# Second attention of a graph network: the edge weight's share of the value as a VectorE term instead of a one-row product

## The chip, the cores and the metric

The kernel runs on one core of a Trainium2 chip. The metric is the device time of one launch in microseconds (us). The program is hand-ordered: each engine (PE = TensorE, PEld = its weight loads, DVE = VectorE, ACT = ScalarE, POOL = GpSimd, SP = SyncE, which issues most DMAs) runs its own list of instructions, and semaphores tie the lists together.

## What is computed

The reference runs two graph layers over 50,000 nodes with 128 features and 12,500 edges. The change lies in the second of two transformer convolutions of the first network. Cut to what matters:

```python
q = (h @ Wq + bq).reshape(n, HEADS, C)
k = (h @ Wk + bk).reshape(n, HEADS, C)
v = (h @ Wv + bv).reshape(n, HEADS, C)
e = (edge_attr @ We).reshape(-1, HEADS, C)      # edge_attr: (12500, 1), We: (1, 128)
k_j = k[src] + e
alpha = einsum('ehc,ehc->eh', q[tgt], k_j) / sqrt(C)
a = softmax of alpha over the edges that share a target
msg = (v[src] + e) * a[..., None]
out = segment_sum(msg, tgt)
```

The edge attribute is one number per edge, so `e` is an outer product: the edge's weight times the 128 numbers of We. It enters twice, in the key and in the value.

## The kernel before

The program is a chain of phases with a barrier between them: first dense layer, first attention (from 487 us of the span), second dense layer, second attention (from 1076 to 1400 us), last dense layer, last edge stage. The change touches the second attention alone, `attention(..., l=1)`.

An attention works on the 12,500 edges in 25 chunks (C) of 500 (CH), with features on the 128 partitions and edges along the free axis. Edges are sorted by target. `edge.hd` and `edge.hs` hold, for all 25 chunks, the features at the target and the source of each edge. The second attention has three parts:

1. **The gather pass** (1082.8 to about 1256 us). For chunk k POOL issues four indirect DMAs (`gather`, L1134) that fetch the source rows into `rows` (a ring of U = 4 buffers). PE turns them (`turn`, L210), ACT copies them into `hs[:, k]` (L1364), PE multiplies by Wq and Wk (`query_key`, L1291 and L1292), ACT evicts the query (L1369), and DVE makes the key with its edge share and the product of query and key (`product`, L1416 and L1421). PE sums the products per head into one accumulating bank (`score`, L1297). PE also makes the value (`value`): the product with Wv (L1305) and, onto it, the product of We with the chunk's weights (L1306), which has one contracted row, `ew`, a [1, 500] row loaded by SP. ACT evicts the value with its bias over `hs[:, k]` (L1373).
2. **The softmax** across all edges (about 1256 to 1275 us), a serial chain of DVE instructions that begins with the scan at L1493 and needs the last score.
3. **The output pass** (1275 to 1400 us): weights spread to 128 partitions, times the value, running sums, gate, skip and the store. The value is read from `hs[:, k]`, since EARLY = 25 for l = 1.

The order in each engine's list comes from `steps(n, stages)`: at step t it runs every stage with its lag, so a stage with lag 1 handles chunk t - 1. In the gather pass PE's list is

```python
steps(C, [(0, turn), (1, query_key), (2, score), (1, value)])
```

so step t turns chunk t, but makes key, query and value of chunk t - 1. DVE's list has `product(t)`, then a piece of set-up work for the softmax (`prepare`, for t = 1 to 14; `count`, for t = 15 to 17). SP's list for chunk k is: `load_index` (L1228, the 2 KB of node numbers that POOL's gather k needs), `load_weights_wide` (L1236, the chunk's weights broadcast to 128 partitions, 250 KB, into the ring `ewb` of 4 slots), `store_hd` (L1231, 250 KB), `load_weight` (L1241, the [1, 500] row). `load_weights_wide(k)` first waits until slot k - 4 has been read. SP works through its list in order, so whatever stands behind a waiting entry waits too; `hold` is the wait:

```python
def load_weights_wide(k):
    q = k % U
    hold(sp, ph.seen, m.kj, made(k - U))
    sp.dma_start(ewb[:, q], weight_row(a, k).to_broadcast([128, CH])).then_inc(ewb_loaded[q], 16)
```

In the traces `att_run_cont<-in_edge_weight` is the wide load (ewb is a view of run_cont), `att_dx` is the key kj, `att_prod` its product with the query, and `att_bank` any of the eight PSUM banks. Both attentions have the same names and lines; the stretch tells them apart.

Of the kernel before, what the change touches and what calls it, by code (L numbers as in the profile page):

```python
# [19 lines left out]
ALU = mybir.AluOpType  # L20
# [7 lines left out]
CH = TILE * TILES  # L28
# [16 lines left out]
def made(k):  # L45


    return k + AHEAD + 1
# [67 lines left out]
def hold(sp, seen, sem, value):  # L116

    sp.wait_ge(sem, value)
    sp.sem_inc(seen, 1)
# [1026 lines left out]
def steps(n, stages):  # L1146

    for t in range(min(0, min(lag for lag, _ in stages)), n + max(lag for lag, _ in stages)):
        for lag, stage in stages:
            if 0 <= t - lag < n:  # L1150
                stage(t - lag)
# [20 lines left out]
def attention(nc, a, w, scratch, l, edge):  # L1172
# [4 lines left out]
    U, C = 4, ECHUNK  # L1177
    EARLY = C if l else 10
    with phase(nc, f"att{l}") as ph:
        hd, hs = edge.hd, edge.hs  # L1180
        ew = ph.sb("ew", [1, U, CH])
        qs, prod = ph.sb("qs", [128, 2, CH]), ph.sb("prod", [128, 2, CH])
# [9 lines left out]
        vs, pv = qs, prod  # L1192
        ewb = run_cont[:, :, 0:CH]
        o, sig, dx = (ph.sb(n, [128, 2, CH]) for n in ("o", "sig", "dx"))
        yd = edge.hs
        kj = dx
# [10 lines left out]
        else:  # L1207
            rows = ph.sb("rows", [TILE, U, TILES, D])
        hd_stored, yd_stored = ph.count("hd_stored"), ph.count("yd_stored")
        names = "xT hs qk qs kj prod score weight spread v vs pv o xz gated xo sig dx gx y yn ystats"  # L1210
        m = Group(**{n: ph.stage(n + "_made") for n in names.split()})
        compact, shifted, exps_made = (ph.count(n) for n in ("compact_step", "shifted", "exps_made"))
        counted, rcnt_stored = ph.count("counted"), ph.count("rcnt_stored")
        LAST = C - 1
        with nc.Block() as block:
            @block.sync
            def _(sp):
                ph.start(sp)
                sp.wait_ge(made_first, 1)
                for h in range(HEADS):  # L1220
                    sp.dma_start(cont[32 * h:32 * h + C], compact_flags(scratch)).then_inc(win_loaded, 16)

                def load_index(k):

                    q = k % U
                    if k >= U:
                        hold(sp, ph.seen, idx_loaded[q], 16 * (k // U))
                    sp.dma_start(idx[:, k], index_slot(scratch.src_row if l else scratch.end_index, k * CH)).then_inc(idx_loaded[q], 16)  # L1228

                def store_hd(k):  # L1230
                    sp.dma_start(cols_of(scratch.hdT, k * CH), hd[:, k]).then_inc(hd_stored, 16)  # L1231

                def load_weights_wide(k):
                    q = k % U
                    hold(sp, ph.seen, m.kj, made(k - U))
                    sp.dma_start(ewb[:, q], weight_row(a, k).to_broadcast([128, CH])).then_inc(ewb_loaded[q], 16)  # L1236

                def load_weight(k):
                    q = k % U
                    hold(sp, ph.seen, m.v, made(k - U))  # L1240
                    sp.dma_start(ew[:, q], weight_row(a, k)).then_inc(ew_loaded[q], 16)  # L1241

                def load_cont(k):
                    q = k % U
                    hold(sp, ph.seen, m.yn, made(k - U))
                    if k < U:
                        hold(sp, ph.seen, m.kj, made(LAST))
                    sp.dma_start(run_cont[:, q], cont_window(scratch, k * CH)).then_inc(cont_loaded[q], 16)

                def late_weight(k):  # L1250
                    if k >= EARLY:
                        load_weight(k)

                def late_cont(k):
                    if k >= U:
                        load_cont(k)

                def store_yd(k):
                    hold(sp, ph.seen, m.yn, made(k))
                    sp.dma_start(cols_of(scratch.ydT, k * CH), yd[:, k]).then_inc(yd_stored, 16)  # L1260

                steps(C, [(0, load_index), (0, load_weights_wide)] + [(0, store_hd), (0, load_weight)] * l)
                if l == 0:
                    steps(U, [(0, load_weight)])
                    steps(U, [(0, load_cont)])
                    for k in range(U, EARLY):
                        load_weight(k)
                if l == 1:
                    sp.wait_ge(counted, 1)
                    sp.dma_start(scratch.rcnt.rearrange("o (c e) -> (o c) e", e=CH), bwd[0:C]).then_inc(rcnt_stored, 16)  # L1270
                steps(C, [(0, load_cont), (4, store_yd)] if l else [(0, late_weight), (0, late_cont)])
                for q in range(U):
                    sp.wait_ge(moved[q], 16 * TILES * len(range(q, C, U)))
                if l == 1:
                    sp.wait_ge(hd_stored, 16 * C)
                    sp.wait_ge(yd_stored, 16 * C)

            @block.tensor
            def _(pe):
# [19 lines left out]
                def value(k):  # L1299
                    if EARLY <= k < EARLY + 2:  # L1300
                        pe.wait_ge(m.qs, made(LAST))
                    ps = (psE if k < EARLY else psV)[k % 2]
                    pe.wait_ge(ew_loaded[k % U], 16 * (k // U + 1))
                    pe.wait_ge(m.vs, made(k - 2))
                    pe.matmul(ps[:, 0:CH], w.Wv[:, l], hs[:, k], start=True, stop=False)  # L1305
                    pe.matmul(ps[:, 0:CH], w.We[:, l], ew[:, k % U], start=False, stop=True).then_inc(m.v, 1)  # L1306

# [94 lines left out]
            def _(dve):  # L1402
# [9 lines left out]
                def product(k):  # L1412
# [8 lines left out]
                    dve.scalar_tensor_tensor(out=prod[:, s], in0=kj[:, s], scalar=w.bk[:, l:l + 1], in1=qs[:, s],  # L1421
                                             op0=ALU.add, op1=ALU.mult).then_inc(m.prod, 1)

                def across(values, z, keep, op):

                    after(dve.transpose(tr[:, 0], values[:, 0:32]))
                    after(dve.transpose(tr[:, 1], values[:, CH - 32:CH]))
                    after(dve.tensor_tensor(tr[:], tr[:], near_mask[:] if op == ALU.max else near[:], ALU.add if op == ALU.max else ALU.mult))
                    first, none = (ALU.add, -BIG) if op == ALU.max else (ALU.mult, 0.0)
                    after(dve.tensor_tensor_scan(z[:, 0, 30::-1], keep[:, 0, 31:0:-1], tr[:, 0, 31:0:-1], none, first, op))  # L1430
                    after(dve.tensor_tensor_scan(z[:, 1, 1:32], keep[:, 1, 0:31], tr[:, 1, 0:31], none, first, op))
                    after(dve.transpose(tr[:, 0], z[:, 0]))
                    after(dve.transpose(tr[:, 1], z[:, 1]))
                    return tr[:, 1, 31:32], tr[:, 0, 0:1]
# [49 lines left out]
                        dve.reciprocal(bwd[:], run[:]).then_inc(counted, 1)  # L1484

                before = None
                steps(C, [(0, product), (0, prepare)] + [(0, count)] * l)

                score = psS[:, 0:CH]
                dve.wait_ge(m.score, made(LAST))  # L1490
# [21 lines left out]
                def weigh(k):  # L1512
                    s = k % 2
                    dve.wait_ge(m.spread, made(k))
                    dve.wait_ge(m.vs, made(k))
                    dve.tensor_tensor(pv[:, s], psB[s][:, 0:CH], hs[:, k] if k < EARLY else vs[:, s], ALU.mult).then_inc(m.pv, 1)

                def total(k):
# [336 lines left out]
```

## Time and profile before

| | |
|---|---|
| median of 3 runs | 2256.45 us (2256.12 to 2262.39) |
| the profiled execution | 2257.61 us, its span 2255.8 us, granted TensorE clock 0.951 |
| busy share of the span | PE 87%, DVE 73%, ACT 58%, POOL 52% |
| gather pass of the second attention | 1082.8 to 1256 us |
| POOL's gathers there (L1134) | x100, 1286 ns each, 1.58 us from one to the next |
| products with one contracted row there (L1306) | x50, 630 ns each |

A matmul of f32 data appears as two instructions, so x50 is 25 products. A duration is one instruction's; the time beside an arrow (<-) is the idle time that ended with that release. Idle time of an engine costs only where nothing else is as late.

### The profile page before, as it was taken

How to read it: one execution, taken by the hardware profiler on the slowest of the kernel's cores; microseconds unless marked ns; L12 is line 12 of the kernel's file. 1: busy time of each engine (PE TensorE's matmuls, PEld its weight loads, DVE VectorE, ACT ScalarE, POOL GpSimd, SP SyncE). 2: the span in 40 equal slices, each digit the busy share in tenths (PEclk: the TensorE clock that was granted, in tenths of full speed). 3: DMA queues.
4: the chain of work that ended last, by engine and by line, in shares of the span. 5: the costliest groups of instructions: out<-in, count | busy, mean ns of one | idle time of the engine just before them, and what ended most of it. 6: DMA issues, size and time to landing. Idle time of an engine off the chain costs nothing. (4 is left out here: it accounts for less than half of the span.)

```text
span 2255.8 us, 32073 instructions
## 1 busy us (share of the span) xinstructions
PE 1955.5 (87%) x7584; PEld 1106.6 (49%) x7584; DVE 1643.9 (73%) x3493; ACT 1311.6 (58%) x2509; POOL 1181.4 (52%) x919
## 2 busy tenths in 40 slices
PE   3899999989996888888588696699999999699997
PEld 2444444444332444444233232477777777355554
DVE  6799999967798899999223698577777775355553
ACT  3688888852222677777233111677777775466562
POOL 7466566428840433333688000555555556578885
PEclk9899999999898999999789799799999999799999
DMA  7888888744122999999444133999999995744441
GB/s 173 249 260 254 257 254 254 235 142 96 33 50 79 321 363 356 374 368 327 125 122 115 47 101 103 287 317 331 310 324 323 317 326 188 176 119 117 115 107 30
DMA packets 289533, 476.30 MB, mean 211 GB/s; under 512 B 85811, under 2 KB 162496, under 8 KB 289223
## 3 DMA queue, kind: packets, MB, share of 16 engines
q1 hardware_dynamic: 239124, 441.09, 61.9%
q0 software_dynamic: 46400, 33.03, 7.2%
q8 instruction: 64, 1.05, 0.2%
q14 instruction: 121, 0.99, 0.1%
q10 hardware_dynamic: 3824, 0.13, 0.1%
HBM read 272.11 MB, written 202.60 MB: 210 GB/s over the span
## 5 line engine op out<-in xcount | busy, mean ns | idle before, releaser
L389 POOL DMA_INDIRECT first_x<-in_x,first_index x200 | 261.2, 1306 | 160.8 <-ACT first_xn L583 83.6
L1007 POOL TENSOR_TENSOR last_xh<-last_xin,last_hin 125x512 f32<-125x512 f32 x100 | 127.1, 1272 | 213.4 <-DMA last_xin<-in_x 197.1
L785 POOL DMA_INDIRECT second_entry<-node_map,second_si x100 | 130.8, 1308 | 198.4 <-DVE second_src_row L800 171.7
L1091 PE MATMUL last_psH<-last_g,W2a 128*128 128x500 f32 x400 | 187.8, 592 | 21.1 <-DVE last_hid L1053 20.9
L1100 PE MATMUL last_psO<-W2b,last_hid 128*125 128x128 f32 x1600 | 190.9, 273 | 0.0
L1100 PEld LDWEIGHTS last_psO<-W2b,last_hid 128*125 128x125 f32 x1600 | 182.5, 188 | 0.9 <-issue 0.9
L203 ACT ACTIVATE last_xn<-last_x,last_nb,last_rstd 125x128 f32<-125x128 f32 x400 | 164.0, 487 | 0.1
L543 PE MATMUL first_psW<-first_h,W_in 128*128 128x500 f32 x300 | 154.1, 596 | 0.0
L1386 ACT ACTIVATE att_sig<-att_bank,gate_b 128x500 f32<-128x500 f32 x50 | 33.9, 678 | 196.4 <-PE att_bank L1329 196.4
L1142 POOL DMA_INDIRECT out<-elast_o,elast_ends x100 | 126.6, 1266 | 39.8 <-issue 39.2
L1134 POOL DMA_INDIRECT att_rows<-h_rows,att_idx x100 | 128.6, 1286 | 36.1 <-issue 33.6
L1142 POOL DMA_INDIRECT node_map<-att_er,att_idx x100 | 128.2, 1282 | 34.9 <-issue 29.6
L1416 DVE SCALAR_TENSOR_TENSOR att_dx<-att_run_cont,We_col,att_bank 128x500 f32<-128x500 f32 x50 | 36.6, 733 | 149.9 <-PE att_bank L1292 141.5
L856 PE MATMUL second_psZ<-second_h,gate_h 128*128 128x500 f32 x200 | 105.0, 607 | 47.0 <-DVE second_y L811 30.1
L1012 POOL TENSOR_TENSOR last_x1b<-last_x,b2b 125x512 f32<-125x512 f32 x100 | 136.4, 1364 | 12.8 <-DVE last_o L1060 12.8
L583 ACT ACTIVATE first_xn<-first_x,first_nb,first_rstd 125x128 f32<-125x128 f32 x300 | 131.0, 490 | 19.7 <-DVE first_nb L476 19.5
L191 DVE BATCH_NORM_STATS2 first_st<-first_x 125x6 f32<-125x256 f32 x300 | 113.0, 419 | 23.9 <-DMA first_x<-in_x 20.7
L210 PEld LDWEIGHTS first_psT<-ident,first_xn 125*128 125x128 f32 x600 | 76.8, 145 | 93.4 <-issue 85.8
L551 PE MATMUL first_psZ<-first_h,gate_h 128*128 128x500 f32 x200 | 102.7, 595 | 19.6 <-DVE first_y L496 18.3
L991 ACT ACTIVATE last_hid<-last_psH,b2u 128x500 f32<-128x500 f32 x100 | 67.3, 673 | 80.0 <-PE last_psH L1091 79.7
L759 ACT ACTIVATE second_y<-second_psZ,gate_b 128x500 f32<-128x500 f32 x100 | 67.5, 675 | 75.2 <-PE second_psX L857 46.5
L1053 DVE TENSOR_SCALAR last_hid<-last_psH,b2u 128x500 f32<-128x500 f32 x100 | 73.1, 731 | 46.7 <-PE last_psH L1091 46.7
(288 smaller groups left out, 5110.5 us busy)
## 6 DMA issues: line engine op xcount, KB each, us to landing
hT<-first_h SPq DMA_DIRECT2D x100, 250.0 KB, 2.5
yT<-first_y SPq DMA_DIRECT2D x100, 250.0 KB, 2.9
second_yin<-yT SPq DMA_DIRECT2D x50, 500.0 KB
second_hin<-hT SPq DMA_DIRECT2D x50, 500.0 KB
yT<-second_y SPq DMA_DIRECT2D x50, 500.0 KB
last_yin<-yT SPq DMA_DIRECT2D x50, 500.0 KB
first_x<-in_x SPq DMA_DIRECT2D x100, 224.0 KB
h_rows<-second_rows SPq DMA_DIRECT2D x50, 448.0 KB, 8.1
```

The costliest lines, as they stand in the source:

```text
L191: last = dve.bn_stats(st[:, t:t + 2].rearrange("p t s -> p (t s)"), x[:, t:t + 2].rearrange("p t f -> p f t"))
L203: last = act.activation(xn[:, j], x[:, j], ACT.Relu, bias=nb[:, j:j + 1], scale=rstd[:, j:j + 1])
L389: pool.indirect_dma_start(x[:, to % X, j], None, a["x"], bass.IndirectOffsetOnAxis(index[:, end, r % 2, j:j + 1], 0), bounds_check=NODES - ...
L543: pe.matmul(psW[k % 2][:, 0:CH], w.W_in[:], h0[:, k % 2], start=True, stop=True).then_inc(m.w_in, 1)
L583: last = act.activation(xn[:, k % 2, j], x[:, k % X, j], ACT.Identity, bias=nb[:, s, i:i + 1], scale=rstd[:, s, i:i + 1])
L785: pool.indirect_dma_start(entry[:, q], None, scratch.node_map, bass.IndirectOffsetOnAxis(si[:, q], 0), bounds_check=NODES - 1, oob_is_err= ...
L1007: pool.tensor_tensor(xh[:, q % 4], xin[:, q], hin[:, q], ALU.add).then_inc(m.xh, 1)
L1012: pool.tensor_tensor(x1b[:, q], x1[:, q], w.b2b[:].rearrange("p (o f) -> p o f", o=1).to_broadcast([TILE, TILES, D]), ALU.add).then_inc(m. ...
L1091: last = pe.matmul(psH[h][:, 0:CH], w.W2a[:, 0, h * 128:(h + 1) * 128], g[:, q % 2], start=True, stop=True)
L1100: last = pe.matmul(psO[q % 2][0:TILE, j * D:(j + 1) * D], tile_cols(hid[:, q % 4, h], j, False), w.W2b[:, h], start=(h == 0), stop=(h == 1))
L1134: pool.indirect_dma_start(rows[:, j], None, table, bass.IndirectOffsetOnAxis(index[:, j:j + 1], 0), bounds_check=table.shape[0] - 1, oob_i ...
L1142: pool.indirect_dma_start(table, bass.IndirectOffsetOnAxis(index[:, j:j + 1], 0), rows[:, j], None, bounds_check=table.shape[0] - 1, oob_i ...
```

## The change

For l = 1 the value is only the product with Wv. DVE adds the edge's share afterwards, in place in `hs[:, k]`: `term(k)` multiplies the wide weights by We's column and adds the evicted value. It stands in DVE's list with lag 2. The one-row loads are no longer issued in this attention. A slot of `ewb` is now read twice, so the wait ahead of the wide load (and ahead of the first loads of `run_cont` in the output pass) is on `term` in place of `kj`.

```diff
                 def load_weights_wide(k):
                     q = k % U
-                    hold(sp, ph.seen, m.kj, made(k - U))
+                    hold(sp, ph.seen, m.term if l else m.kj, made(k - U))
                     sp.dma_start(ewb[:, q], weight_row(a, k).to_broadcast([128, CH])).then_inc(ewb_loaded[q], 16)
...
                     if k < U:
-                        hold(sp, ph.seen, m.kj, made(LAST))
+                        hold(sp, ph.seen, m.term if l else m.kj, made(LAST))
...
-                steps(C, [(0, load_index), (0, load_weights_wide)] + [(0, store_hd), (0, load_weight)] * l)
+                steps(C, [(0, load_index), (0, load_weights_wide)] + [(0, store_hd)] * l)
...
                     ps = (psE if k < EARLY else psV)[k % 2]
+                    pe.wait_ge(m.vs, made(k - 2))
+                    if l == 1:
+                        pe.matmul(ps[:, 0:CH], w.Wv[:, l], hs[:, k], start=True, stop=True).then_inc(m.v, 1)
+                        return
                     pe.wait_ge(ew_loaded[k % U], 16 * (k // U + 1))
-                    pe.wait_ge(m.vs, made(k - 2))
                     pe.matmul(ps[:, 0:CH], w.Wv[:, l], hs[:, k], start=True, stop=False)
                     pe.matmul(ps[:, 0:CH], w.We[:, l], ew[:, k % U], start=False, stop=True).then_inc(m.v, 1)
...
+                def term(k):
+                    dve.wait_ge(m.vs, made(k))
+                    dve.scalar_tensor_tensor(out=hs[:, k], in0=ewb[:, k % U], scalar=w.We_col[:, l:l + 1], in1=hs[:, k],
+                                             op0=ALU.mult, op1=ALU.add).then_inc(m.term, 1)
...
-                steps(C, [(0, product), (0, prepare)] + [(0, count)] * l)
+                steps(C, [(0, product), (0, prepare)] + [(2, term), (0, count)] * l)
...
                     dve.wait_ge(m.vs, made(k))
+                    if l == 1:
+                        dve.wait_ge(m.term, made(k))
                     dve.tensor_tensor(pv[:, s], psB[s][:, 0:CH], hs[:, k] if k < EARLY else vs[:, s], ALU.mult).then_inc(m.pv, 1)
```

SP's list in the gather pass, from the store of chunk 3 on, before the change (att1_idx is the index load of the next chunk, att1_run_cont the wide weights, att1_ew the one-row weights):

```order
L1231 DMA hdT<-hd 128x500
L1241 DMA att1_ew<-in_edge_weight1 1x500
L1228 DMA att1_idx<-src_row 125x4
L1236 DMA att1_run_cont<-in_edge_weight1 128x500
L1231 DMA hdT<-hd 128x500
L1241 DMA att1_ew<-in_edge_weight1 1x500
L1228 DMA att1_idx<-src_row 125x4
```

And with the change, the same place:

```order
L1231 DMA hdT<-hd 128x500
L1228 DMA att1_idx<-src_row 125x4
L1236 DMA att1_run_cont<-in_edge_weight1 128x500
L1231 DMA hdT<-hd 128x500
L1228 DMA att1_idx<-src_row 125x4
L1236 DMA att1_run_cont<-in_edge_weight1 128x500
```

The one-row loads are gone; every index load still stands behind the wide load of the chunk before it, and that one now waits for `term`.

DVE's list at the end of the gather pass with the change (L1419 and L1424 are the new lines of the key and of its product with the query, L1429 is `term`, L1501 the first scan of the softmax):

```order
L1419 SCALAR_TENSOR_TENSOR att1_dx<-att1_run_cont,We_col,att1_bank3 128x500
L1424 SCALAR_TENSOR_TENSOR att1_prod<-att1_dx,bk,att1_qs 128x500
L1429 SCALAR_TENSOR_TENSOR hs<-att1_run_cont,We_col,hs 128x500
L1419 SCALAR_TENSOR_TENSOR att1_dx<-att1_run_cont,We_col,att1_bank2 128x500
L1424 SCALAR_TENSOR_TENSOR att1_prod<-att1_dx,bk,att1_qs 128x500
L1429 SCALAR_TENSOR_TENSOR hs<-att1_run_cont,We_col,hs 128x500 x3
L1501 SCALAR_TENSOR_TENSOR att1_fwd<-att1_apart,att1_bank4 128x500
```

Before, the scan followed directly on the last product of key and query; now the terms of the last three chunks stand between them.

## Rows read from the trace of the kernel before

**Rows 1.** Engines' busy time over the gathers; then clock, DMA share, GB/s.

```profile
1082.80:1241.50 158.70, 128.26 (x323) 55.40 (x324) 49.87 (x83) 54.55 (x69) 128.52 (x100) 0.86 0.45 120
```

**Rows 2.** Groups of the gather pass, 1082 to 1256 us, shapes apart: busy, mean ns | idle.

```profile
L1134 POOL DMA_INDIRECT att_rows<-h_rows,att_idx x100 | 128.6, 1286 | 36.1 <-issue 33.6 <-PE att_bank L210 1.2 <-DMA att_idx<-src_row 1.2
...
L1306 PE MATMUL att_bank<-att_ew,We 1*128 1x500 f32 x50 | 27.5, 630 | 0.0
...
L1416 DVE SCALAR_TENSOR_TENSOR att_dx<-att_run_cont,We_col,att_bank 128x500 f32<-128x500 f32 x25 | 18.3, 731 | 127.0 <-PE att_bank L1292 127.0
...
L1471 DVE TENSOR_TENSOR att_sel<-blocks,att_ind 128x640 f32<-128x640 f32 x5 | 4.1, 819 | 0.0
```

**Rows 3.** Timeline of POOL: first gather of chunks 0, 5 and 24.

```profile
1082.79 1.28 POOL L1134 DMA_INDIRECT att_rows<-h_rows,att_idx  x1 [5.88 <-issue]
...
1114.39 1.27 POOL L1134 DMA_INDIRECT att_rows<-h_rows,att_idx  x1 [0.30 <-issue]
...
1235.31 1.49 POOL L1134 DMA_INDIRECT att_rows<-h_rows,att_idx  x1 [0.30 <-issue]
```

**Rows 4.** Timeline of PE: turning of chunks 0, 3, 9, 23 and 24.

```profile
1090.93 1.10 PE L210 MATMUL att_bank<-ident,att_rows 125*128 125x125 f32 x4 [21.81 <-DMA att_rows<-h_rows,att_idx]
...
1111.35 1.10 PE L210 MATMUL att_bank<-ident,att_rows 125*128 125x125 f32 x4 [2.73 <-DMA att_rows<-h_rows,att_idx]
...
1149.41 1.10 PE L210 MATMUL att_bank<-ident,att_rows 125*128 125x125 f32 x4 [1.88 <-DMA att_rows<-h_rows,att_idx]
...
1237.24 0.65 PE L210 MATMUL att_bank<-ident,att_rows 125*128 125x125 f32 x4 [0.50 <-DMA att_rows<-h_rows,att_idx]
...
1243.59 0.65 PE L210 MATMUL att_bank<-ident,att_rows 125*128 125x125 f32 x4 [1.31 <-DMA att_rows<-h_rows,att_idx]
```

**Rows 5.** Timeline of DVE in the gather pass and at its end.

```profile
1115.33 0.73 DVE L1416 SCALAR_TENSOR_TENSOR att_dx<-att_run_cont,We_col,att_bank 128x500 f32<-128x500 f32 x1 [7.33 <-PE att_bank L1292]
...
1116.76 1.19 DVE L1444 TENSOR_TENSOR_SCAN att_hflag<-att_cont 128x499 f32<-128x499 f32 x1
...
1153.98 0.74 DVE L1416 SCALAR_TENSOR_TENSOR att_dx<-att_run_cont,We_col,att_bank 128x500 f32<-128x500 f32 x1 [6.89 <-PE att_bank L1292]
...
1239.68 0.73 DVE L1416 SCALAR_TENSOR_TENSOR att_dx<-att_run_cont,We_col,att_bank 128x500 f32<-128x500 f32 x1 [4.02 <-PE att_bank L1292]
...
1247.61 0.73 DVE L1416 SCALAR_TENSOR_TENSOR att_dx<-att_run_cont,We_col,att_bank 128x500 f32<-128x500 f32 x1 [6.42 <-PE att_bank L1292]
...
1248.38 0.74 DVE L1421 SCALAR_TENSOR_TENSOR att_prod<-att_dx,bk,att_qs 128x500 f32<-128x500 f32 x1
...
1253.07 0.74 DVE L1421 SCALAR_TENSOR_TENSOR att_prod<-att_dx,bk,att_qs 128x500 f32<-128x500 f32 x1
...
1255.98 1.20 DVE L1493 TENSOR_TENSOR_SCAN att_fwd<-att_apart,att_bank 128x500 f32<-128x500 f32 x1 [2.16 <-PE att_bank L1297]
```

**Rows 6.** Timeline of SP's queue: index loads 0, 5, 24; neighbours of 0; wide load 6.

```profile
1079.03 0.30 SPq L1228 DMA_DIRECT2D att_idx<-src_row  x1
1079.45 0.36 SPq L1236 DMA_DIRECT2D att_run_cont<-in_edge_weight  x1
...
1080.41 0.25 SPq L1241 DMA_DIRECT2D att_ew<-in_edge_weight  x1
...
1103.65 0.27 SPq L1228 DMA_DIRECT2D att_idx<-src_row  x1
...
1116.16 0.36 SPq L1236 DMA_DIRECT2D att_run_cont<-in_edge_weight  x1
...
1227.26 0.27 SPq L1228 DMA_DIRECT2D att_idx<-src_row  x1
```

**Rows 7.** Last edge stage, SP and POOL: a 250 KB load, an index load, its gather.

```profile
1988.71 0.43 SPq L1613 DMA_DIRECT2D elast_rcnt<-rcnt  x1
...
1989.62 0.27 SPq L1601 DMA_DIRECT2D elast_si<-src_row  x1
...
1994.84 1.47 POOL L1134 DMA_INDIRECT elast_x<-x_rows,elast_si  x1 [5.02 <-DMA elast_si<-src_row]
```

More of the change, by code:

```diff
@@ L1209, in attention @@
         hd_stored, yd_stored = ph.count("hd_stored"), ph.count("yd_stored")
-        names = "xT hs qk qs kj prod score weight spread v vs pv o xz gated xo sig dx gx y yn ystats"
+        names = "xT hs qk qs kj prod score weight spread v vs pv o xz gated xo sig dx gx y yn ystats term"
         m = Group(**{n: ph.stage(n + "_made") for n in names.split()})
```

## The prediction

> **What bounds the kernel now.** I read the stage table first, then the groups of the gather pass, then four timelines side by side. Over the gathers of the second attention no engine but POOL is full [rows 1]: POOL is busy 128.52 of 158.70 us, and what is left is the 0.30 us between two of its issues [rows 3]. PE looks as busy (128.26 us), but its turnings are released by the landing of gathers [rows 4], and DVE sits idle 127.0 us in total before its keys [rows 2]. So the pace is POOL's: four gathers of 1286 ns and their gaps, 6.3 us per chunk, from 1082.79 (chunk 0) to 1235.31 (chunk 24) [rows 3]. PE, DVE and ACT follow and catch up. Only after the last gather has landed is their own time on the path: 1243.59, when chunk 24 is turned, to 1255.98, when the softmax starts [rows 4, 5].
>
> POOL keeps this pace because its indices are there in time. Index load 5 is issued at 1103.65 [rows 6] for a gather that starts at 1114.39 [rows 3], 10.7 us ahead; index load 24 at 1227.26 for 1235.31, 8.1 us ahead. In the whole pass a landing of indices is named for 1.2 us of POOL's idle time [rows 2]. That margin is the place to look at: the index load of chunk k stands in SP's list behind the wide load of chunk k - 1, and the change alters what that one waits for.
>
> **What the change takes away.** 25 products with one contracted row, 27.5 us of PE in all, 1.1 us per chunk [rows 2]. PE waits for gathers in this pass, so 23 of them lay in time that PE had anyway: worth nothing. The one of step 24 and the one of step 25 come after the last gather, 2.2 us. The 25 small loads cost SP about 0.3 us each, and SP waits most of the time: nothing.
>
> **What it adds on DVE.** 25 terms of the size of a key, 0.73 us with a gap of 0.04, about 0.8 us each. DVE has room in the pass, so 22 are covered. The terms of the last three chunks stand between the last product of key and query and the first scan: 3 x 0.77 = 2.3 us. Before, that stretch was 1253.07 + 0.74 = 1253.81 to 1255.98, 2.2 us of waiting for PE [rows 5]. The terms take the place of that wait, so of the 2.2 us saved on PE only the product ahead of the last key counts: 1.1 - 0.1 = 1.0 us off the path.
>
> POOL could pay for the terms too. One of its gathers in rows 3 took 1.49 us where the others took 1.27; 0.2 us for each of 25 terms would be 5 us, none is the other bound, and I take 0, since over 100 gathers the mean is only 1286 ns [rows 2] although 25 products of key and query, with the same two inputs in SBUF, already run there. The Trainium skill speaks against the change here: in "SBUF — State Buffer", section "SBUF: two separate sides", a VectorE instruction with two SBUF inputs and a GpSimd instruction that reads SBUF exclude each other for their whole length. Read at its worst it would put 25 x 0.77 = 19 us into the sum, and the mean of 1286 ns does not bear that out.
>
> **What it moves: the release of the index loads.** Before, wide load k - 1 waited for key k - 5, and index load k followed (with the small load between). Now wide load k - 1 waits for term k - 5. Term k - 5 has lag 2, so DVE runs it behind product k - 3, and product k - 3 needs the key matmul that PE does in step k - 2, behind the turning of chunk k - 2, which waits for gather k - 2. So gather k can't start before gather k - 2 has landed and gone through PE, DVE, SP and a load. That is a loop over two chunks; its length from start of one gather group to start of the next but one:
>
> - start of the four gathers to the turning: 1082.79 to 1090.93 and 1235.31 to 1243.59 [rows 3, 4], 8.1 and 8.3; I take 8.2.
> - turning to the key on DVE: 1111.35 to 1115.33, 1149.41 to 1153.98, 1243.59 to 1247.61 give 4.0, 4.6, 4.0; 1237.24 to 1239.68, after only 0.50 us of idle time, gives 2.4 [rows 4, 5]. The long ones follow idle times of 1.3 to 2.7 us, after which the granted clock of PE is at the low one of its two levels (1.2 of 2.4 GHz) for some microseconds. In the loop PE will idle longer than that, so I take 4.1.
> - key and product: 1247.61 to 1248.38 + 0.74, 1.5 us [rows 5]. Term: 0.8.
> - SP: a wide load goes out 0.1 us after its release (1115.33 + 0.73 to 1116.16) [rows 5, 6], and what comes behind the wide load and the store goes out 1.0 us later (1079.45 to 1080.41) [rows 6].
> - issue of the index load to the gather. Behind little traffic: 1079.03 to 1082.79, 3.8 us [rows 3, 6]. Behind loads of 250 KB, as here: 1989.62 to 1994.84, 5.2 us, though with more loads following [rows 7]. I take 4.8, nearer to the second, whose traffic ahead is like this one's.
>
> Sum: 8.2 + 4.1 + 1.5 + 0.8 + 0.1 + 1.0 + 4.8 = 20.5 us for two chunks, where POOL needs 12.6. For the last term a page has a price of its own: "DMA: Bandwidth & Descriptors", section "Anatomy of one DMA — SWDGE (gpsimd) path", in the Trainium skill gives about 2.0 us fixed plus bytes over 436 GB/s (for POOL's own path). Behind 500 KB that is an estimate of 3.2 us, a loop of 18.9 and a time of about 2323; the rows' 3.8 and 5.2 are longer.
>
> Now the pass. Index loads 0 to 4 go out before any such wait. Chunk 5 is the first in the loop: turning 3 at 1111.35, key 2 at 1115.33, DVE free of product and set-up scan at 1116.76 + 1.19 = 1117.95 [rows 5], then 0.8 + 0.1 + 1.0 + 4.8: gather 5 starts at about 1124.7 instead of 1114.39. The odd chunks then lead, each even one follows by POOL's 6.3 us. From 5 to 23 are nine loops: 9 x 20.5 = 184.5. Set-up work stands ahead of the term in six of them, at most 0.8 us each [rows 2]; I take 3 in all. Gather 23 starts at 1312, gather 24 at 1318.5, against 1235.31: 83 us later.
>
> At the end I take off the 1.0 us above and another 1.0, as the last chunk follows on chunk 23 with PE awake. Softmax and output pass are unchanged; their first loads wait for the last term, with about 20 us of softmax as cover. Sum: 83 - 2 = 81 us. The profiled execution had 2257.6 us, so 2338.7; the median of the runs lies 1.2 us below it, so **2338**.
>
> **The rivals.**
> 1. *The margin is enough* (the side opposite to mine). The index loads are prefetched, so a later release is hidden, and only the end of the pass moves: 2257 - 1 to 2 = 2255 us, no measurable change. It holds if the release moves by less than the margin minus the load's own time, 8.1 - 4.8 = 3.3 us. For it: the 1.2 us in rows 2. Against it: lag 2 moves the release by two chunks, 12.6 us, and the term itself. 5%.
> 2. *A short loop.* The same mechanism, with PE at its full level (2.4 for 4.1) and a 3.8 us load: 17.8 us per loop, gather 5 at 1123.7, nine loops and 3 us, then 6.3: gather 24 at 1293, 58 us late, 2314. For it: chunks now come in pairs, and the second of a pair finds PE awake; against it: the first of a pair sets the loop, after a long idle time. In full or in part 17%.
> 3. *The port.* No index load late, but every term stops a gather for its own length: 19 us, less 2: 2274. The skill's rule on two SBUF inputs gives it; the 1286 ns speak against it. 2%.
> 4. *The loop as I add it up*, 19 to 22 us: 2325 to 2356. 76%.
>
> **The numbers.** The predicted time is that of case 4. The low end reaches down to case 2, 2308; the high end has the longer key (4.6), a load of 6 us and the full set-up, +5 +12 +2, so 2356. That leaves out case 1, case 3 and the tails, about 15%. A run of this kernel can tell about 0.3%, 6.8 us, from no change. Slower by more than that: cases 2, 3, 4 = 0.95. Within: case 1, 0.04. Faster by more: 0.01, since nothing after the last gather offers 6.8 us.
>
> **What would show it.** In the profile after: POOL's idle time before the gathers with a landing of `att_idx` named, near 80 us against 1.2; gathers in groups of eight, 12.6 us of work and then a gap of about 8 us; index load 5 issued near 1120, not 1103.65; the last gather group starting near 1318; SP waiting for DVE's new line; a lower mean clock than 0.86 in the pass. The end, from the last turning to the first scan, shorter than 12.4 us by 1 to 3, with three terms in a row ahead of the scan. Output pass still about 125 us. I am wrong if POOL keeps its 0.30 us gaps (case 1), if the gathers themselves lengthen (case 3), or if the gap per pair is under 6 us (case 2).

## The result and the profile after

The changed kernel takes 2321.69 us (median of 4 runs, 2315.9 to 2328.35), the kernel before 2256.28 us beside it; the ratio is 1.0277 with a 95% interval of 1.0247 to 1.0307. The forecast was 2338, within 2308 to 2356.

The page of the changed kernel, its span and the group of gathers that now heads POOL's idle time (busy, mean ns | idle before, releaser):

```profile
span 2320.4 us, 31938 instructions
...
L1134 POOL DMA_INDIRECT att_rows<-h_rows,att_idx x100 | 128.4, 1284 | 108.1 <-DMA att_idx<-src_row 67.3
```

The gathers last what they did (1284 ns for 1286 [rows 2]). What grew is the idle time ahead of them, from 36.1 to 108.1 us, and the releaser is the landing of indices: 67.3 us where it was 1.2. The waits of the stretch from 1075 to 1330 us (total, times, longest):

```profile
DVE att_dx L1419 <- PE att_bank L1292: 180.5, 25, 29.3
...
PE att_bank L210 <- DMA att_rows<-h_rows,att_idx: 129.0, 19, 21.9
POOL att_rows L1134 <- DMA att_idx<-src_row: 67.3, 11, 8.1
POOL att_rows L1134 <- issue: 40.5, 88, 8.1
```

Of the ten long gaps one is booked under "issue". The wait behind these gaps stands in SP's queue. Its longest before (1075 to 1260 us), and then after (1075 to 1330 us; total, times, longest):

```profile
SPq L119 <- DVE att_dx L1416: 111.6, 22, 20.5
```

```profile
SPq L119 <- DVE hs L1429: 211.5, 22, 30.4
```

L119 is the line of `hold`; what it waits for there is now the term, and no longer the key. Engines over the gathers, from the first to the last (answering to [rows 1]; busy, then clock, DMA share, GB/s):

```profile
1086.30:1315.40 229.10, 113.89 (x273) 54.06 (x274) 62.24 (x101) 54.70 (x68) 127.08 (x99) 0.74 0.29 80
```

The stretch is 229.1 us long for the same work, and the granted clock is 0.74 in place of 0.86. POOL's timeline, answering to [rows 3]: the first gather of chunks 0, 5, 7 and 23, with the idle time ahead of each:

```profile
1086.30 1.28 POOL L1134 DMA_INDIRECT att_rows<-h_rows,att_idx  x1 [6.02 <-issue]
...
1124.04 1.71 POOL L1134 DMA_INDIRECT att_rows<-h_rows,att_idx  x1 [6.44 <-DMA att_idx<-src_row]
...
1144.89 1.28 POOL L1134 DMA_INDIRECT att_rows<-h_rows,att_idx  x1 [7.93 <-DMA att_idx<-src_row]
...
1304.36 1.27 POOL L1134 DMA_INDIRECT att_rows<-h_rows,att_idx  x1 [6.86 <-DMA att_idx<-src_row]
```

From chunk 5 on there is such a gap before every odd chunk, and the even chunk follows at POOL's own pace: eight gathers, then 6.4 to 8.1 us of nothing. From 1124.04 to 1304.36 are nine loops over two chunks, 20.04 us each, where POOL alone needs 12.6.

One turn of the loop can be read from four timelines. First DVE: the key of chunk 2, its product, a piece of set-up, then term 0 (answering to [rows 5]):

```profile
1115.97 0.74 DVE L1419 SCALAR_TENSOR_TENSOR att_dx<-att_run_cont,We_col,att_bank 128x500 f32<-128x500 f32 x1 [4.46 <-PE att_bank L1292]
1116.74 0.74 DVE L1424 SCALAR_TENSOR_TENSOR att_prod<-att_dx,bk,att_qs 128x500 f32<-128x500 f32 x1
1117.40 1.19 DVE L1452 TENSOR_TENSOR_SCAN att_hflag<-att_cont 128x499 f32<-128x499 f32 x1
1118.63 0.74 DVE L1429 SCALAR_TENSOR_TENSOR hs<-att_run_cont,We_col,hs 128x500 f32<-128x500 f32 x1
```

Then SP, released by that term: wide load 4, the store, index load 5 (answering to [rows 6]):

```profile
1119.45 0.33 SPq L1236 DMA_DIRECT2D att_run_cont<-in_edge_weight  x1
1119.84 0.43 SPq L1231 DMA_DIRECT2D hdT<-hd  x1
1120.37 0.27 SPq L1228 DMA_DIRECT2D att_idx<-src_row  x1
```

The term ends at 1119.37, the wide load goes out at 1119.45, the index load at 1120.37 and its gather starts at 1124.04, 3.67 us later. Then PE, which turns chunks 3, 5 and 6 (answering to [rows 4]):

```profile
1113.51 0.65 PE L210 MATMUL att_bank<-ident,att_rows 125*128 125x125 f32 x4 [2.39 <-DMA att_rows<-h_rows,att_idx]
...
1132.59 1.09 PE L210 MATMUL att_bank<-ident,att_rows 125*128 125x125 f32 x4 [8.98 <-DMA att_rows<-h_rows,att_idx]
1139.17 0.65 PE L210 MATMUL att_bank<-ident,att_rows 125*128 125x125 f32 x4 [0.68 <-DMA att_rows<-h_rows,att_idx]
```

Chunk 5 finds PE after 8.98 us of idle time, and its four turnings take 1.09 us, chunk 6 after 0.68 us, and they take 0.65. The granted clock from a turning to the key behind it is 0.50 to 0.57 for the first chunk of all ten pairs (4.2 to 4.6 us), and 1.00 for chunk 6 (2.44 us). At the end of the pass, DVE again: the last product, the three terms in a row and the first scan.

```profile
1325.54 0.74 DVE L1424 SCALAR_TENSOR_TENSOR att_prod<-att_dx,bk,att_qs 128x500 f32<-128x500 f32 x1
1326.19 2.03 DVE L1429 SCALAR_TENSOR_TENSOR hs<-att_run_cont,We_col,hs 128x500 f32<-128x500 f32 x3
1328.14 1.19 DVE L1501 TENSOR_TENSOR_SCAN att_fwd<-att_apart,att_bank 128x500 f32<-128x500 f32 x1
```

**Where the 65 us are.** First to last start of a gather: 157.5 us before (1082.79 to 1240.26), 229.1 after, +71.6. Start of the last gather to the first scan: 15.7 before (to 1255.98), 12.7 after (1315.4 to 1328.14), -3.0. Together +68.6. The two profiled spans differ by 64.6, because two stretches that the change does not touch differ between the executions: the changed one enters the pass 3.5 us later, and its last dense layer is shorter. The outputs of that layer, before and then after (first and last start):

```profile
L1060 DVE TENSOR_TENSOR last_o<-last_psO,last_x1b x100: 673/691/693, 1454.5 to 1916.5; 125x512 f32<-125x512 f32 x100
```

```profile
L1060 DVE TENSOR_TENSOR last_o<-last_psO,last_x1b x100: 674/691/693, 1526.8 to 1981.5; 125x512 f32<-125x512 f32 x100
```

462.0 and 454.7 us. In the profiled runs of e1 to e8 below, whose code there is the same, that stretch took between 452.6 and 461.7 us, so a difference of a few us in the total says nothing; the pass is compared in the trace.

### The profile page after: what moved, and what is told of

Its sections match the earlier page's. It is cut to its first block and busy times, and to the rows that moved or that the text cites. A ratio compares the mean times of both kernels' runs of the same rounds, so it can differ in the third digit from the quotient of the medians.

```text
span 2320.4 us, 31938 instructions
## 1 busy us (share of the span) xinstructions
PE 1946.4 (84%) x7534; PEld 1106.7 (48%) x7534; DVE 1666.8 (72%) x3518; ACT 1312.9 (57%) x2509; POOL 1181.1 (51%) x919
## 5 line engine op out<-in xcount | busy, mean ns | idle before, releaser
L785 POOL DMA_INDIRECT second_entry<-node_map,second_si x100 | 128.6, 1286 | 198.6 <-DVE second_src_row L800 168.2
L1091 PE MATMUL last_psH<-last_g,W2a 128*128 128x500 f32 x400 | 190.8, 600 | 11.4 <-DVE last_hid L1053 11.3
L1134 POOL DMA_INDIRECT att_rows<-h_rows,att_idx x100 | 128.4, 1284 | 108.1 <-DMA att_idx<-src_row 67.3
L1419 DVE SCALAR_TENSOR_TENSOR att_dx<-att_run_cont,We_col,att_bank 128x500 f32<-128x500 f32 x50 | 36.7, 735 | 203.5 <-PE att_bank L1292 191.1
L1142 POOL DMA_INDIRECT out<-elast_o,elast_ends x100 | 126.0, 1260 | 40.2 <-issue 39.6
L1012 POOL TENSOR_TENSOR last_x1b<-last_x,b2b 125x512 f32<-125x512 f32 x100 | 136.0, 1360 | 12.7 <-DVE last_o L1060 12.7
L210 PE MATMUL att_bank<-ident,att_rows 125*128 125x125 f32 x100 | 21.4, 352 | 129.1 <-DMA att_rows<-h_rows,att_idx 129.0
L486 DVE TENSOR_SCALAR first_xn<-first_x,first_rstd,first_nb 125x128 f32<-125x128 f32 x300 | 104.6, 435 | 11.1 <-PE first_psT L210 7.4
```

The source lines that it names most:

```text
L785: pool.indirect_dma_start(entry[:, q], None, scratch.node_map, bass.IndirectOffsetOnAxis(si[:, q], 0), bounds_check=NODES - 1, oob_is_err= ...
L1012: pool.tensor_tensor(x1b[:, q], x1[:, q], w.b2b[:].rearrange("p (o f) -> p o f", o=1).to_broadcast([TILE, TILES, D]), ALU.add).then_inc(m. ...
L1091: last = pe.matmul(psH[h][:, 0:CH], w.W2a[:, 0, h * 128:(h + 1) * 128], g[:, q % 2], start=True, stop=True)
L1134: pool.indirect_dma_start(rows[:, j], None, table, bass.IndirectOffsetOnAxis(index[:, j:j + 1], 0), bounds_check=table.shape[0] - 1, oob_i ...
L1142: pool.indirect_dma_start(table, bass.IndirectOffsetOnAxis(index[:, j:j + 1], 0), rows[:, j], None, bounds_check=table.shape[0] - 1, oob_i ...
```

## The experiments

The theory: the index load of chunk k is caught in SP's list behind a wide load that now waits for a term two chunks of work later, so gather k waits for gather k - 2. Rivals: the terms themselves (DVE's work, or a port shared with POOL), the removed products (PE idles and its clock sinks), or a fixed charge of the late wait.

**e1, index loads two chunks earlier.** Everything else of the change stays.

```diff
-                steps(C, [(0, load_index), (0, load_weights_wide)] + [(0, store_hd)] * l)
+                steps(C, [(-2 * l, load_index), (0, load_weights_wide)] + [(0, store_hd)] * l)
```

> The changed kernel with one thing moved: in SP's list of the second attention the index load of chunk k stands two chunks earlier, behind the wide load of chunk k - 3 (which waits for term k - 7) instead of k - 1. Terms, removed products and the later wait of the wide loads all stay. Theory (the index load is caught behind the later wait, a loop over two chunks of 20.0 us): the loop is open again, POOL goes back to 6.3 us per chunk and 0.30 us gaps, the time is that of the kernel before less 1 to 2 us, 2252 to 2257. Rival port (a term with two inputs in SBUF stops POOL's gathers): gathers stay slow, up to 19 us over the kernel before, about 2273. Rival DVE work (the terms themselves or the late weights set the pace): stays above 2300.

Measured: 2256.54 us, median of 12, against 2257.35 of the kernel before beside it; ratio 0.9995 (0.9973 to 1.0018). The gathers and the engines over the pass:

```profile
L1134 POOL DMA_INDIRECT att_rows<-h_rows,att_idx x100 | 130.0, 1300 | 35.6 <-issue 34.1 <-DMA att_idx<-src_row 1.5
```

```profile
1081.10:1240.10 159.00, 105.94 (x274) 48.32 (x275) 62.85 (x101) 55.32 (x68) 128.80 (x100) 0.85 0.44 117
```

The whole loss is gone with one number in the order of SP's list, while all terms run, all one-row products stay away and the wide loads wait for the term as in the changed kernel. The wait for indices is 1.5 us, the clock 0.85. The terms and the missing products are excluded as causes of the 65 us, and with them a clock that sinks because of them. Once the loop is closed, the low clock is a part of its length all the same: turning to key takes 4.46 us in the mean at the low level and 2.44 at the full one, which makes an estimate of 2 us per loop, some 20 of the 71.6 us.

**e2, the late wait alone, in the kernel before.** No term, products and small loads as they were.

```diff
-                    hold(sp, ph.seen, m.kj, made(k - U))
+                    hold(sp, ph.seen, m.prod if l else m.kj, made(k - U + 2 * l))
```

> The kernel before, with only the wait ahead of the wide load moved: in the second attention wide load k waits for the product of query and key of chunk k - 2 (the instruction that a term k - 4 would follow) instead of key k - 4. No term, and the one-row products and loads stay. Theory: the wait alone makes the loss; the loop is that of the changed kernel, 20.0 us, less the term (0.8) and up to 0.3 of set-up work, plus 0.35 for the small load that stands ahead of the index load again, so about 19.3 us against 12.6 for two chunks; ten loops less than the changed kernel's by 0.7 each, but the end of the pass as before (3 us longer): 60 to 68 us over the kernel before, 2316 to 2324. Rival (DVE's terms or the missing products, which let PE's clock sink, make the loss): no change, 2256.

Measured: 2322.92 us, ratio 1.0284 (1.0242 to 1.0325). POOL, first gathers of chunks 3, 5 and 7:

```profile
1110.21 1.50 POOL L1134 DMA_INDIRECT att_rows<-h_rows,att_idx  x1 [6.10 <-DMA att_idx<-src_row]
...
1129.47 1.56 POOL L1134 DMA_INDIRECT att_rows<-h_rows,att_idx  x1 [6.72 <-DMA att_idx<-src_row]
...
1148.79 1.27 POOL L1134 DMA_INDIRECT att_rows<-h_rows,att_idx  x1 [6.75 <-DMA att_idx<-src_row]
```

The first two loops take 19.3 us, as written before the run; from chunk 3 to chunk 23 (1300.72) the ten take 19.05 in the mean. They begin two chunks earlier than in the changed kernel, since here wide load 2 is the first that waits. With e1 this is both directions: the wait makes the loss without the rest of the change, and the rest of the change makes none without the wait.

**e3 and e9, the term's lag 1 and 3.** The same 25 terms, SP's list untouched; only the number of chunks that the loop spans changes.

```diff
-                steps(C, [(0, product), (0, prepare)] + [(2, term), (0, count)] * l)
+                steps(C, [(0, product), (0, prepare)] + [(1, term), (0, count)] * l)
```

(and `(3, term)` for e9)

> The changed kernel with the term's lag 1 in place of 2 (term k - 1 behind product k). SP's list as in the changed kernel. Theory: gather k now hangs on gather k - 3, so the same loop of about 20 us spans three chunks, for which POOL needs 19.0: 0 to 1 us per three chunks, seven or eight times, less 1 to 3 us at the end (two terms instead of three ahead of the scan): 2253 to 2262. Rival port or DVE work: the same 25 terms run, so the time stays near the changed kernel's 2320.

> The changed kernel with the term's lag 3 in place of 2, SP's list unchanged. Theory: gather k now hangs on gather k - 1, so the loop spans one chunk. From the trace of the changed kernel it is 20.0 us for two chunks; nothing in it changes but the chunks it spans, so POOL should gather four, wait about 14 us, and gather again: chunks 5 to 24 are 20 loops of 19.5 to 20 us where POOL needs 6.3, 263 to 273 us, less 3 us at the end: 2516 to 2530 in all. Rival (the loss of the changed kernel is a fixed charge per late wait, or DVE's added work): one more step of lag adds as much as the step from 1 to 2 did, 60 us, 2380.

Lag 1: 2261.93 us, ratio 1.0049 (1.0021 to 1.0076). POOL's rows in the middle of the pass:

```profile
1122.15 1.27 POOL L1134 DMA_INDIRECT att_rows<-h_rows,att_idx  x1 [0.97 <-DMA att_idx<-src_row]
...
1176.24 1.27 POOL L1134 DMA_INDIRECT att_rows<-h_rows,att_idx  x1 [1.38 <-DMA att_idx<-src_row]
...
1217.81 1.27 POOL L1134 DMA_INDIRECT att_rows<-h_rows,att_idx  x1 [2.18 <-DMA att_idx<-src_row]
```

The gaps are 1 to 3 us where there are any, and the gathers take 168.0 us from first to last start, 10.5 more than before. The total is at the upper end of what was written and the pass is past it (at most 8 us more): from chunk 4 (1107.99) to chunk 24 (1245.93) three chunks take 20.7 us, where POOL needs 19.0. About 2 us of the 10.5 are longer gathers (1307 ns for 1286), which e6 explains. The loss of 4.6 us is small but clear of zero.

Lag 3: 2536.14 us, ratio 1.1207 (1.1107 to 1.1307), a little above the 2516 to 2530 expected. First gathers of chunks 5, 6 and 24:

```profile
1132.45 1.27 POOL L1134 DMA_INDIRECT att_rows<-h_rows,att_idx  x1 [12.69 <-DMA att_idx<-src_row]
1152.40 1.27 POOL L1134 DMA_INDIRECT att_rows<-h_rows,att_idx  x1 [13.94 <-DMA att_idx<-src_row]
...
1512.61 1.27 POOL L1134 DMA_INDIRECT att_rows<-h_rows,att_idx  x1 [13.81 <-issue]
```

1132.45 to 1512.61 is 380.2 us for 19 chunks, 20.01 us for one, where the change takes 20.04 for two. So the length of the loop is nearly a constant, and what a chunk takes is that length divided by the chunks it spans: 20.0 (lag 3), 10.0 (lag 2), and for lag 1 6.7 by the constant and 6.9 measured, with POOL's 6.3 as the floor. A fixed charge would have given 2380. The pass of lag 3 is 428.8 us, 271 more than before and within the 263 to 273 written; what was missed is the end, which did not get 3 us shorter (last gather to first scan 16.7 for 15.7).

**e4, the index load ahead of the two large transfers**, behind the same wait.

```diff
                     hold(sp, ph.seen, m.term if l else m.kj, made(k - U))
+                    if l and k + 1 < C:
+                        load_index(k + 1)
                     sp.dma_start(ewb[:, q], weight_row(a, k).to_broadcast([128, CH])).then_inc(ewb_loaded[q], 16)
...
-                steps(C, [(0, load_index), (0, load_weights_wide)] + [(0, store_hd)] * l)
+                if l:
+                    load_index(0)
+                    steps(C, [(0, load_weights_wide), (0, store_hd)])
+                else:
+                    steps(C, [(0, load_index), (0, load_weights_wide)])
```

> The changed kernel with the index load of the next chunk ahead of the wide load and the store, but behind the same wait on the term. Theory: the loop loses the 1.0 us that SP spends on the two large issues. If the large transfers ahead also held up the index load (it took 3.65 us from issue to the gather), that falls toward the 2.9 us of the very first index load of the program (issued at 2.21, its gather at 5.14), another 0.7: ten loops of 20.0 become 19.0 or 18.3, the time 2312 or 2305. Rival (the two large transfers hold up nothing and SP's issue is not in the loop): 2321.

Measured: 2306.91 us, ratio 1.0219 (1.0176 to 1.0262). SP's issues of index load 7, wide load and store, and POOL's gather 7:

```profile
1132.30 0.27 SPq L1228 DMA_DIRECT2D att_idx<-src_row  x1
1132.62 0.33 SPq L1238 DMA_DIRECT2D att_run_cont<-in_edge_weight  x1
1132.99 0.53 SPq L1231 DMA_DIRECT2D hdT<-hd  x1
```

```profile
1135.16 1.53 POOL L1134 DMA_INDIRECT att_rows<-h_rows,att_idx  x1 [6.71 <-DMA att_idx<-src_row]
```

From issue to gather 2.86 us here; the ten first chunks of a pair (5 to 23) took 2.44 to 2.86, median 2.51, against 3.60 to 4.35, median 3.69, in the changed kernel. The loop, from 1115.84 (chunk 5) to 1278.87 (chunk 23), is 18.1 us. That is 1.9 us less than 20.04: the two 250 KB transfers ahead of the index load cost it 0.9 us of SP's issue and about 1.1 us of landing.

**e5, neither product nor term.**

```diff
-                steps(C, [(0, load_index), (0, load_weights_wide)] + [(0, store_hd), (0, load_weight)] * l)
+                steps(C, [(0, load_index), (0, load_weights_wide)] + [(0, store_hd)] * l)
...
+                    if l == 1:
+                        pe.matmul(ps[:, 0:CH], w.Wv[:, l], hs[:, k], start=True, stop=True).then_inc(m.v, 1)
+                        return
```

> The kernel before without the one-row products and their loads, and with nothing in their place: the edge's share of the value is left out of the second attention. Theory: in the gather pass the 23 products of the middle lay in PE's idle time, so the first to the last gather stays at 157.5 us; of the two after the last gather both count now, and PE is awake as in the changed kernel, so last gather to first scan falls from 15.7 to 11 to 13.5 us. In all 2 to 4 us, 2253. Rival (the products set PE's pace in the pass): the pass shortens by up to 25 us.

Measured: 2256.36 us, ratio 0.9999 (0.9976 to 1.0021). The gathers took 159.3 us from first to last start, so the one-row products of the middle were worth nothing. Last gather to first scan is 11.9 us, 3.9 less than before. The 2 to 4 us written for the total don't show in it, in part because the gathers were 1.8 us slower in this execution (see e6).

**e6, every term twice**, on the base of e1. The wait ahead of the wide load is on the second of the two.

```diff
                                             op0=ALU.mult, op1=ALU.add).then_inc(m.term, 1)
+                    dve.wait_ge(m.term, made(k))
+                    dve.wait_ge(m.again, made(k - 2))
+                    dve.scalar_tensor_tensor(out=o[:, k % 2], in0=ewb[:, k % U], scalar=w.We_col[:, l:l + 1], in1=hs[:, k],
+                                             op0=ALU.mult, op1=ALU.add).then_inc(m.again, 1)
```

> The kernel with the index loads two chunks earlier, and every term followed by a second instruction of the same form (wide weights times We plus value) that writes a buffer nobody reads. Theory: DVE has room in the pass; the only cost is at the end, three more instructions of 0.77 us ahead of the first scan less what PE leaves idle there, last gather to first scan 12.6 plus 2 to 4 us. Rival port: each added instruction stops a gather; POOL's mean goes from 1300 ns by as much again as it stands over the 1286 of before (1315) or, at the rule's worst, by 190 ns, the pass by 19 us. Total 2257 to 2261 or, by the rival, 2275.

Measured: 2260.13 us, ratio 1.0009 (0.9987 to 1.0032). Last gather to first scan is 15.0 us, 2.4 more than in e1. The gathers:

```profile
L1134 POOL DMA_INDIRECT att_rows<-h_rows,att_idx x100 | 133.6, 1336 | 36.2 <-issue 34.3 <-DMA att_idx<-src_row 1.8
```

1336 ns against 1300 in e1, 3.6 us over 100 gathers, and the pass is 162.5 us for 159.0. But e5, which has no term at all, shows 1304, and the changed kernel 1284: the number of terms alone does not give the mean. The single gathers do. Two of them, each with what DVE ran when it began:

```profile
1203.10 2.16 POOL L1134 DMA_INDIRECT att_rows<-h_rows,att_idx  x1 [0.30 <-issue]
...
1208.71 1.67 POOL L1134 DMA_INDIRECT att_rows<-h_rows,att_idx  x1 [0.30 <-issue]
```

```profile
1202.98 1.20 DVE L1491 TENSOR_TENSOR_SCAN att_fwd<-att_cont,att_ex 128x500 f32<-128x500 f32 x1
...
1208.50 0.73 DVE L1429 SCALAR_TENSOR_TENSOR hs<-att_run_cont,We_col,hs 128x500 f32<-128x500 f32 x1
```

A gather is 1.27 us long as a rule. The second began with 0.52 us of the term still to run and is 0.40 longer, the first with 1.08 us of the scan to run and is 0.89 longer. So it goes in all eleven traces (1100 gathers of this pass): 96 gathers lasted over 1.30 us, and each began while DVE ran an instruction with two inputs in SBUF (product, term, scan, `att_sel` and the like). In 82 of them over 0.2 us of it were left, and there the gather grew by what was left, less 0.12 us (0.19 for a scan), to within 0.02. In two others what fits is the rest of a TENSOR_SCALAR that overlapped the end of the product. None of the gathers that began while DVE was idle, ran a key (one input in PSUM) or the reciprocal (one input) was long. Where the DVE instruction had begun less than 0.10 us before the gather, the gather kept its 1.27 us, and the DVE instruction grew, by at most 0.06. What this costs depends on how many gathers happen to begin inside such an instruction: about 1.1 us over the pass before, 0.9 with the change, 2.9 in e1, 3.3 in e5, 6.4 here, and nothing in e9, where none does. The 3.5 us between e1 and e6 are the 3.5 us by which the pass is longer. The 190 ns per gather of the worst case are excluded.

**e7, e1 with lag 1.** Both edits in one kernel.

> The kernel with the index loads two chunks earlier, and the term at lag 1: one term fewer ahead of the first scan. Theory: the pass at POOL's pace, last gather to first scan 12.6 less up to 0.8, so 11.8 to 12.6; total 2252 to 2256, which a run can hardly tell from the kernel before. Rival (lag 1 makes DVE wait for the value's eviction in every chunk and so delays the keys): no shorter end, or a longer pass.

Measured: 2259.94 us, ratio 1.0005 (0.9986 to 1.0024), above the 2252 to 2256 written, but the kernel before measured 2258.51 beside e5 to e8. Gathers 158.2 us, last gather to first scan 12.1: the 0.5 us less at the end can't be seen in the total.

**e8, six slots for the wide weights**, with SP's list of the changed kernel.

```diff
-        ewb = run_cont[:, :, 0:CH]
+        W = 6 if l else U
+        ewb = ph.sb("ewb", [128, W, CH]) if l else run_cont[:, :, 0:CH]
...
-                    hold(sp, ph.seen, m.term if l else m.kj, made(k - U))
+                    hold(sp, ph.seen, m.term if l else m.kj, made(k - W))
```

> The changed kernel with six slots for the wide weights in place of four (a ring of its own; the unused one-row buffer gives the room). SP's order is that of the changed kernel, the index load again directly behind the wide load of the chunk before. Theory: the wide load waits for term k - 6, two chunks earlier, so the margin of the index load is back and POOL keeps its pace: 2252 to 2257. Rival (the order in SP's list is what costs, whatever the wait): stays near 2320. With it the first loads of the output pass no longer share the ring, which is hidden either way.

Measured: 2255.32 us, ratio 0.9982 (0.9957 to 1.0008). The index load stands where the change left it, directly behind a wide load, and costs nothing, since that wide load waits two chunks less. So position or wait, either one, opens the loop. Last gather to first scan was 14.3 us here, for 12.7 in e1 with the same instructions. The 1.6 us are the clock: from the last turning to the key behind it the granted clock goes down to 0.50 here, and that takes 4.0 us (1245.66 to 1249.66), where e1 stays at 1.00 and takes 2.4 (1243.58 to 1246.02).

No version that was run is faster than the kernel before by more than its interval.

## Why the prediction was right, and by how much its terms were off

**Cause, place and sign** came out as forecast: the release of the index loads, the loop over two chunks, the pairs of chunks with gaps of about 8 us (measured 6.4 to 8.1), the odd chunks leading, a lower clock, SP waiting for the term, three terms ahead of the scan. That index load 5 went out at 1120.37, as forecast for 1120, is luck: it came 3.0 us sooner after the first gather than forecast (34.1 for 37.1), and this execution entered the pass 3.5 us later. Case 4 holds in mechanism: its loop of 19 to 22 us was 20.04, its total ended 3 us below its lower end of 2325. The forecast was 16 us high in the total, 11.4 us in the pass (83 forecast, 71.6 measured):

- **Issue of the index load to the gather** was the term mis-sized: 4.8 taken, 3.67 measured at chunk 5 and, but for one of 4.35, 3.60 to 3.75 after. Over the ten it is 10.5 us of the 11.4. The misses below, up and down, make up the rest. I took it near the 5.2 us of the last edge stage [rows 7] because of the same traffic ahead; but that row has more loads following, and e4 shows what two 250 KB transfers ahead do by themselves: from about 2.5 to about 3.7 us, 1.1 to 1.2 us. The 3.8 us at the start of this pass was the nearer row. The Trainium skill's page "DMA: Bandwidth & Descriptors", section "Anatomy of one DMA — SWDGE (gpsimd) path", has 2.0 us plus bytes over 436 GB/s, for POOL's own path. The share by bytes, an estimate of 1.15 us for 500 KB, agrees with that difference; its fixed part is below the 2.5 us that e4 shows up to the start of the gather.
- **Turning to key**: 4.1 taken, 4.3 measured at chunk 5 (1132.59 to 1136.92 on DVE), 4.46 in the mean of the nine loops: 0.36 us too short, nine times, about 3 us the other way.
- **Start of the loop**: gather 5 came 37.7 us after the first gather (1086.30 to 1124.04), 41.9 forecast. 1.1 us of it is the term above. Turning 3 came 1.4 us sooner after the first gather than before, and PE was at its full level, 2.5 us to the key for 4.0. The forecast had copied both from the trace of before. Gather 3 landed later in the two kernels whose wide load 4 goes out after the first key (start to turning 9.6 us before, 9.9 in e5) than in the others (8.2 to 8.4), so the transfers that are absent at that moment are the likely reason; no run changes them alone.
- **Gather to turning**: 8.2 taken, 8.22 in the mean of nine loops (8.55 at chunk 5). Key and product, term, SP's issues: 3.4 taken, 1.43 + 1.74 = 3.2 measured. **Set-up work**: 3 us taken, 3.8 measured, in six loops. With the terms above the nine loops add up to the measured 20.04 each.
- **The end of the pass**: -2 forecast, -3.0 measured. Of it 1.6 us are the clock from the last turning to the key behind it (2.4 us for 4.0), for which 1.0 had been taken, and e8 shows that this differs between kernels with the same instructions there. The removed products with PE awake gave 11.9 us (e5), the terms put back 0.8 (e1: 12.7).
- **The products in the middle**: forecast worth nothing, and e5 shows nothing.
- **The rest of the total** is no part of the change: in this execution the pass began 3.5 us later and the last dense layer was 7.3 us shorter.
- **Sums of the prediction.** Case 2 leaves out the 2 us at the end, so its sum is 2312, not 2314; the high end adds up to 2357. The margin of 8.1 us in case 1 is that of chunk 24; the smallest was 7.1 (index load 20 at 1202.92, its gather at 1210.03). None of these changes the forecast.

**The rivals.** Case 1 (the margin is enough) fell: 67.3 us of named waiting. Case 2, the short loop, had the right size for the load, and its 3.8 us; but PE was at its low level at the first chunk of every pair (0.50 to 0.57), so its loop of 17.8 us was not reached. Case 3, the port, fell as the cause and as priced: e1 has all terms and a pass of 159.0 us against 157.5, where the Trainium skill's rule in "SBUF — State Buffer", section "SBUF: two separate sides", read at its worst would put 19 us. What the prediction did not see behind the mean of 1286 ns is that the exclusion this page states is there all the same (e6). The gather of 1.49 us at 1235.31 [rows 3] is one case of it: a product with 0.34 us to run was on DVE when it began. It is cheap because a gather pays only when it begins inside such an instruction. And it is one-sided: where the page has whichever starts first keep the port "for the whole instruction", a gather that started first lengthened DVE's instructions by 0.06 us at most. The sum by the DMA page, 2323, lay nearer to the measured 2321.69 than mine did. That is in part luck: its load of 3.2 us is 0.55 below the measured mean, which makes some 5 us over ten, and the last dense layer, the late entry and the other terms happened to offset that.

## What to carry to other kernels

Where a ring slot gets a second, later reader, the wait ahead of its next load moves, and with it everything that stands behind that load in the same queue: list those entries and their margins before pricing the instruction itself. A small prefetch that the pacing engine depends on belongs ahead of entries that wait, or at a distance of its own; here a distance of two chunks, or two more slots, was worth 65 us. A wait that closes a loop costs, per chunk, the loop's length divided by the chunks it spans, less the pace of the slowest engine, so one chunk of lag more or less can turn 5 us into 65 or 275.

## What was not expected of the hardware

An index load of 2 KB took about 2.5 us from SP's issue to the start of the gather with nothing directly ahead of it (e4), and about 3.7 us behind 500 KB that were issued up to 0.9 us earlier (the changed kernel).

The gathers' mean length on POOL moved between 1272 (e9) and 1336 ns (e6) among kernels with the same 100 gathers in this pass; single ones took up to 2.23 us (in e5). The reason is in the traces: an indirect gather that begins while DVE is inside an instruction with two inputs in SBUF lasts longer by what is left of it, less 0.12 us (82 gathers, to within 0.02 us). DVE's keys and its reciprocal, with at most one input in SBUF, lengthened none. A DVE instruction that had begun less than 0.10 us before a gather lengthened none either, and grew by 0.06 us at most itself.
